# A quarter block of rows subtracted by GpSimd in four instructions of 128x512 instead of one of 128x2048

## The chip, the cores and the metric

The kernel runs on one core of one Trainium2 chip. A core has TensorE (PE in the profile, its weight loads PEld), VectorE (DVE), ScalarE (ACT), GpSimd (POOL) and SyncE (SP), which here only issues transfers. The metric is the time of one execution on the device in microseconds (us), lower is better. The profile shows one execution on the one core that is used.

## The reference, cut to what matters

```python
x = x + _L0_xattn_ref(_layernorm(x), ctx_4096)    # the stage that fills the time
x = x + _L0_attn_ref(_layernorm(x), Wq, bq, Wk, bk, Wv, bv)
x = x + _L0_ffn_ref(_layernorm(x), ...)

def _L0_xattn_ref(query, key):                    # query (1, 256, 2048), key (1, 25088, 2048)
    a = jnp.einsum('bqd,bkd->bqk', query, key)
    e = jax.nn.softmax(a, axis=-1)
    c = jnp.einsum('bqk,bkd->bqd', e, key)
```

All is float32. The cross-attention reads its 25088 context rows twice in effect: once as keys (with the feature axis on the partitions) and once as values (rows on the partitions).

## The kernel before

**Splitting.** Each float32 operand of TensorE is split in a high part (a cast to fp32r) and a low part (the operand minus its high part), and each product is three matmuls: high by high, low by high, high by low (lines L960 to L962).

**Blocks.** The context is walked in 49 blocks of 512 rows with a running softmax. A block has two uses, and each has its own tiles:

- *Scores.* The block comes as `quart` (two halves `h` of 4 transfers of 512 KB each). For each of 16 chunks of 128 features, DVE transposes to `tr` (L733), ACT casts to `ch_hi` (L517), DVE subtracts to `ch_lo` (L737), and PE does 6 matmuls (2 tiles of 128 queries, 3 products each). `tr`, `ch_hi` and `ch_lo` are rings of 4 slots; a slot of `ch_hi`/`ch_lo` is written again when PE has used it.
- *Weighted rows.* The same block comes again as `raw`, in 4 pieces of 512 features (1024 KB each) through 2 buffers. ACT casts piece `j` to `nat_hi` (L540), and GpSimd subtracts to `nat_lo` (L459, the changed line). PE multiplies the transposed probabilities with them in 8 steps of 12 matmuls; DVE adds each step's result to `acc` (L775). The 8 steps use 2 PSUM banks in turn, so the third step waits until DVE has added the first.

**Order.** The order is written by hand. PE does the weighted rows of a block in the middle of the next block's scores, after chunk 6. On ACT the four casts of pieces stand after chunk 10 (three of them) and after chunk 11 (the last). DVE runs 3 chunks ahead: between its subtractions it transposes, takes the maximum of the scores (L754, L757) as soon as it gets to it, and subtracts for the probabilities (L667); then it rescales (L765, L767) and adds (L775). `following` says which chunk is transposed behind which subtraction: chunk 8, the first of the second half of `quart`, behind the subtraction of chunk 6.

**Transfers.** All of them but one pair stand in one SP queue, in program order, and each waits at its head:

```python
for j in range(2):
    sp.wait_ge(nat_ready[j + 2], turn.times(1, 1))
    load_rows(j, rows_src(j))
if not turn.first and not turn.last:
    second_half()
```

`nat_ready[j]` is what GpSimd's subtraction of piece `j` increments. So the load of `raw` piece 1 of the next block (L318), and behind it in the queue the four loads of the second half of `quart` (L325), wait for GpSimd's subtraction of piece 3. The second half waits for the transpose of chunk 15 too.

**GpSimd's other work.** In the first 16 rounds of two blocks GpSimd also adds up `Wq` over groups of heads: one load and, after the second block's piece 3, three additions of 128x512 (L472, L473, L475) and a store. Every second block of the first 33 thus has these three behind its piece 3.

Of the kernel before, what the change touches and what calls it, by code (L numbers as in the profile page):

```python
# [5 lines left out]
F32 = mybir.dt.float32  # L6
U32 = mybir.dt.uint32
ALU = mybir.AluOpType
# [20 lines left out]
def perceiver_block(nc, x, ctx, wq, bq, wk, bk, wv, bv, w_base, b_base, w_gate, lora_a, lora_b, out):  # L29
# [21 lines left out]
    KT = KB // P  # L51
# [34 lines left out]
    with ExitStack() as stack:  # L86
        def sem(name):
            return stack.enter_context(nc.semaphore(name))
# [10 lines left out]
        def put(at, name, shape, dt=F32):  # L99
            return nc.alloc_sbuf_tensor_at(name, shape, dt, offset=at)  # L100
# [15 lines left out]
        raw = put(at_raw, "raw", [P, 2, KT, BANK])  # L116
        quart = put(at_quart, "quart", [P, 2, RG, HALF])
        nat_hi = put(at_hi, "nat_hi", [P, PIECES, KT, BANK], F32R)
        nat_lo = put(at_lo, "nat_lo", [P, PIECES, KT, BANK], F32R)
# [102 lines left out]
        nat_ready = [sem(f"nat_ready{j}") for j in range(PIECES)]  # L222
# [84 lines left out]
        def in_pairs(eng, work, start=0, end=PAIRS):  # L307
            with eng.Fori(start, end) as i:
                for step in range(2):
                    work(Turn(i, step))  # L310
# [129 lines left out]
        @block.gpsimd  # L440
        def _(pool):
            pool.memset(ident[:, :], 0.0).then_inc(consts_set, 1)
            pool.memset(ones[:, :], 1.0).then_inc(consts_set, 1)
            pool.iota(iota8[:, :], [[1, EXPERTS]], base=0, channel_multiplier=0,
                      allow_small_or_imprecise_dtypes=True).then_inc(consts_set, 1)

            for parity in range(2):
                pool.memset(neg_max[:, parity, :], -LOWEST).then_inc(max_ready, 1)
            pool.memset(denom[:, :], 0.0).then_inc(denom_ready, 1)
            pool.wait_ge(consts_set, 3)  # L450
            pool.affine_select(out=ident[:, :], in_=ident[:, :], compare_op=ALU.not_equal, fill=1.0,
                               base=0, pattern=[[-1, P]], channel_multiplier=1).then_inc(consts, 1)
            for t in range(TT):
                pool.memset(acc[:, t, :], 0.0).then_inc(acc_updated, 1)

            def lo_piece(j, ready):

                pool.wait_ge(nat_hi_ready, ready)
                pool.tensor_tensor(nat_lo[:, j], raw[:, j % 2], nat_hi[:, j].bitcast(F32), ALU.subtract).then_inc(nat_ready[j], 1)  # L459

            def split_block(turn):
                for j in range(PIECES):
                    lo_piece(j, turn.times(PIECES, j + 1))

            split_block(FIRST)
            with pool.Fori(0, DC) as i:
                pool.dma_start(wq_in[:], wq[bass.ds(i * P, P)].rearrange("p d h -> p (d h)")).then_inc(wq_loaded, 16)
                for step in range(2):
                    split_block(Turn(i, step))
                w4 = wq_in[:].rearrange("p (n j) -> p n j", j=REP)  # L470
                pool.wait_ge(wq_loaded, i * 16 + 16)
                pool.tensor_tensor(w4[:, :, 0], w4[:, :, 0], w4[:, :, 1], ALU.add).then_inc(wq_half, 1)  # L472
                pool.tensor_tensor(w4[:, :, 2], w4[:, :, 2], w4[:, :, 3], ALU.add).then_inc(wq_half, 1)  # L473
                pool.wait_ge(wq_half, i * 2 + 2)
                pool.tensor_tensor(wq_out[:], w4[:, :, 0], w4[:, :, 2], ALU.add).then_inc(wq_summed, 1)  # L475
                pool.wait_ge(wq_summed, i + 1)
                pool.dma_start(wq_dram[bass.ds(i * P, P)], wq_out[:]).then_inc(wq_stored, 16)
                pool.wait_ge(wq_stored, i * 16 + 16)
            in_pairs(pool, split_block, DC, PAIRS)
            for turn in REST:  # L480
                split_block(turn)
            for j in range(PIECES):
                lo_piece(j, NB * PIECES + j + 1)
            pool.wait_ge(wq_stored, 16 * DC)

            pool.wait_ge(qkv_done, 3 * TT)
            pool.memset(v_t[:, :, :, :], 0.0).then_inc(v_zeroed, 1)
            pool.wait_ge(v_zeroed, 1)
            for j in range(2):
                pool.memset(v_t[DH * j:DH * (j + 1), :, :, (KVH + 1) * j + KVH], 1.0).then_inc(v_zeroed, 1)  # L490
# [712 lines left out]
```

## Time and profile before

| what | value |
|---|---|
| device time, median of 3 runs | 2737.11 us (2726.85 to 2743.08) |
| span of the profiled execution | 2735.8 us |
| PE busy | 2517.3 us, 92% |
| DVE busy | 1834.0 us, 67% |
| ACT busy | 1120.2 us, 41% |
| POOL busy | 1018.9 us, 37% |
| chain that ended last | PE 67%, DVE 15%, issue 8%, ACT 5%, DMA 3% |
| `nat_lo` on POOL (L459) | 200 instructions, 921.7 us |

The profiled execution's own device time is not listed apart from the others; its span, 2735.8 us, lies inside the range of the three times. Matmul records overlap, so PE's 92% does not mean that it works at its peak.

### The profile page before, as it was taken

What the parts mean: (1) busy time and instruction counts of PE and PEld (TensorE: products, weight loads), DVE (VectorE), ACT (ScalarE), POOL (GpSimd) and SP (SyncE); (2) the same over time, 40 slices, a digit from 0 to 9 for tenths busy, and PEclk for the clock granted to TensorE, in tenths of its full rate; (3) what the DMA queues carried; (4) which work ended last, traced back from release to release, by engine and by line L of the source; (5) the groups of instructions that cost most, each with busy time, mean ns of one, the idle gap of its engine ahead of it and who ended that gap; (6) DMA issues with size and microseconds to landing.
All of it is one profiled execution on the core that took longest, in us unless ns stands there. A gap on an engine that the chain in (4) does not pass through costs nothing.

```text
span 2735.8 us, 34584 instructions
## 1 busy us (share of the span) xinstructions
PE 2517.3 (92%) x11342; PEld 2044.4 (75%) x11342; DVE 1834.0 (67%) x2668; ACT 1120.2 (41%) x1569; POOL 1018.9 (37%) x296
## 2 busy tenths in 40 slices
PE   5999999999999999999999999999999999996789
PEld 3777777777777777777777777777777777765677
DVE  7767667676766767676675766767576676572568
ACT  3444344443444444444444444444344444331423
POOL 3254443535435353443534444242433435220000
PEclk8999999999999999999999999999999999998579
DMA  9767778687776867767676866767677676658237
GB/s 218 191 179 188 183 196 193 170 202 189 185 178 197 193 177 195 186 180 188 188 198 174 203 172 177 176 169 182 171 180 172 179 174 169 174 138 120 39 67 149
DMA packets 377510, 476.08 MB, mean 174 GB/s; under 512 B 48707, under 2 KB 265795, under 8 KB 374853
## 3 DMA queue, kind: packets, MB, share of 16 engines
q1 hardware_dynamic: 373894, 454.68, 68.1%
q0 software_dynamic: 3584, 20.97, 2.3%
q8 instruction: 20, 0.33, 0.1%
q14 instruction: 12, 0.10, 0.0%
HBM read 467.74 MB, written 7.86 MB: 174 GB/s over the span
## 4 chain that ended last, share of the span: by engine, by line
PE 67%; DVE 15%; issue 8%; ACT 5%; DMA 3%; SPq 1%; POOL 0%; ACTq 0%; DVEq 0%
PE ps L960 22%; PE ps L962 21%; PE ps L961 21%; DVE ch_lo L737 10%; ACT ch_hi L517 2%; ACT nat_hi L540 2%; DVE blk_max L754 1%; DMA raw<-in_L_attn_Wv_dram 1%; DVE tr L733 1%; DMA raw<-in_ctx_dram 1%; PE ps L969 1%; DMA q_t<-qk_dram 1%; SPq L325 1%; PE ps L990 1%; PE ps L1135 1%
## 5 line engine op out<-in xcount | busy, mean ns | idle before, releaser
L459 POOL TENSOR_TENSOR nat_lo<-raw,nat_hi 128x2048 fp32r<-128x2048 f32 x200 | 921.7, 4609 | 1269.5 <-ACT nat_hi L540 1269.5
L737 DVE TENSOR_TENSOR ch_lo<-tr,ch_hi 128x512 fp32r<-128x512 f32 x848 | 782.0, 927 | 168.0 <-ACT ch_hi L517 165.6
L960 PE MATMUL ps<-ch_hi,xt_hi 128*128 128x512 f32 x1696 | 697.0, 411 | 136.8 <-DVE ch_lo L737 134.3
L517 ACT CAST ch_hi<-tr 128x512 fp32r<-128x512 f32 x848 | 516.2, 620 | 743.3 <-DVE tr L733 372.6
L775 DVE SCALAR_TENSOR_TENSOR acc<-acc,alpha,ps 128x512 f32<-128x512 f32 x392 | 292.6, 747 | 583.2 <-PE ps L962 583.0
L962 PE MATMUL ps<-ch_hi,xt_lo 128*128 128x512 f32 x1696 | 675.4, 398 | 0.0
L961 PE MATMUL ps<-ch_lo,xt_hi 128*128 128x512 f32 x1696 | 675.1, 398 | 0.0
L540 ACT CAST nat_hi<-raw 128x2048 fp32r<-128x2048 f32 x208 | 397.3, 1910 | 620.4 <-PE ps L962 353.1
L960 PE MATMUL ps<-nat_hi,pt_hi 128*128 128x512 f32 x1568 | 610.9, 390 | 1.4 <-DVE pt_lo L667 1.4
L962 PE MATMUL ps<-nat_hi,pt_lo 128*128 128x512 f32 x1568 | 610.6, 389 | 0.0
L961 PE MATMUL ps<-nat_lo,pt_hi 128*128 128x512 f32 x1568 | 610.5, 389 | 0.0
L733 DVE STREAM_TRANSPOSE tr<-quart 128x512 f32<-128x512 f32 x848 | 588.6, 699 | 3.2 <-DMA quart<-in_ctx_dram 1.8
L960 PEld LDWEIGHTS ps<-ch_hi,xt_hi 128*128 128x128 f32 x1696 | 327.7, 193 | 240.4 <-DVE ch_lo L737 171.7
L962 PEld LDWEIGHTS ps<-ch_hi,xt_lo 128*128 128x128 f32 x1696 | 326.5, 193 | 72.0
L961 PEld LDWEIGHTS ps<-ch_lo,xt_hi 128*128 128x128 f32 x1696 | 328.3, 194 | 64.4 <-issue 0.7
L960 PEld LDWEIGHTS ps<-nat_hi,pt_hi 128*128 128x128 f32 x1568 | 294.8, 188 | 62.8 <-DVE pt_lo L667 1.6
L961 PEld LDWEIGHTS ps<-nat_lo,pt_hi 128*128 128x128 f32 x1568 | 294.8, 188 | 61.2
L962 PEld LDWEIGHTS ps<-nat_hi,pt_lo 128*128 128x128 f32 x1568 | 294.7, 188 | 61.2
L546 ACT ACTIVATE probs<-ps,neg_max 128x512 f32<-128x512 f32 x98 | 67.5, 689 | 98.0 <-DVE neg_max L757 98.0
L754 DVE TENSOR_REDUCE blk_max<-ps 128x1 f32<-128x512 f32 x98 | 65.4, 667 | 4.5 <-PE ps L962 4.4
L667 DVE TENSOR_TENSOR pt_lo<-ps,pt_hi 128x512 fp32r<-128x512 f32 x98 | 66.9, 683 | 1.6 <-ACT pt_hi L501 1.6
L969 PE MATMUL ps<-ident,probs 128*128 128x128 f32 x392 | 59.4, 274 | 3.0 <-ACT probs L546 1.9
(125 smaller groups left out, 913.4 us busy)
## 6 DMA issues: line engine op xcount, KB each, us to landing
quart<-in_ctx_dram SPq DMA_DIRECT2D x392, 512.0 KB, 9.0
raw<-in_ctx_dram SPq DMA_DIRECT2D x196, 1024.0 KB, 5.1
wq_in<-in_L_attn_Wq_dram POOLq DMA_DIRECT2D x16, 1024.0 KB, 5.5
quart<-in_L_ffn_W_base_dram SPq DMA_DIRECT2D x32, 512.0 KB, 8.6
wq_dram<-wq_out POOLq DMA_DIRECT2D x16, 256.0 KB, 8.6
raw<-in_L_attn_Wk_dram SPq DMA_DIRECT2D x4, 1024.0 KB, 5.3
raw<-wq_dram SPq DMA_DIRECT2D x4, 1024.0 KB, 5.4
raw<-in_L_attn_Wv_dram SPq DMA_DIRECT2D x4, 1024.0 KB, 16.7
```

The source lines that it names most:

```text
L459: pool.tensor_tensor(nat_lo[:, j], raw[:, j % 2], nat_hi[:, j].bitcast(F32), ALU.subtract).then_inc(nat_ready[j], 1)
L517: act.copy(ch_hi[:, c % RING_CH, :], tr[:, c % RING_TR, :]).then_inc(chunk_hi, 1)
L540: act.copy(nat_hi[:, j], raw[:, j % 2]).then_inc(nat_hi_ready, 1)
L546: act.activation(probs[:, q, :], ps[:, SCORE_BANK + TT * new + q, :], ACT.Exp, bias=neg_max[:, new, q:q + 1], accum_out=row_sum[:, q:q + 1 ...
L733: dve.transpose(tr[:, c % RING_TR, :].rearrange("p (r i) -> p r i", i=SQ), src).then_inc(chunk_transposed, 1)
L737: dve.tensor_tensor(ch_lo[:, c % RING_CH, :], tr[:, c % RING_TR, :], ch_hi[:, c % RING_CH, :].bitcast(F32), ALU.subtract).then_inc(chunk_s ...
L754: dve.tensor_reduce(blk_max[:, q:q + 1], ps[:, SCORE_BANK + TT * new + q, :], AX.X, ALU.max, negate=True).then_inc(blkmax_ready, 1)
L775: dve.scalar_tensor_tensor(piece, piece, alpha[:, q:q + 1], ps[:, out_bank(v, turn.over), :], ALU.mult, ALU.add).then_inc(acc_updated, 1)
L960: pe.matmul(out_, a_hi, b_hi, start=start, stop=False)
L961: pe.matmul(out_, a_hi, b_lo, start=False, stop=False)
L962: return pe.matmul(out_, a_lo, b_hi, start=False, stop=stop)
L969: last = pe.transpose(ps[:, bank, a * P:(a + 1) * P], src, ident[:, :])
```

## The change

```diff
             def lo_piece(j, ready):
 
                 pool.wait_ge(nat_hi_ready, ready)
-                pool.tensor_tensor(nat_lo[:, j], raw[:, j % 2], nat_hi[:, j].bitcast(F32), ALU.subtract).then_inc(nat_ready[j], 1)
+                for t in range(KT):
+                    last = pool.tensor_tensor(nat_lo[:, j, t], raw[:, j % 2, t], nat_hi[:, j, t].bitcast(F32), ALU.subtract)
+                last.then_inc(nat_ready[j], 1)
```

`KT` is 4. The same elements are read and written, and one semaphore increment follows the last of the four, as it followed the one. All 200 subtractions of GpSimd become 800. Nothing else is changed; behind this place the line numbers of the changed kernel are higher by 2.

On GpSimd (POOL), before, the end of the round of two blocks that also has the additions for `Wq`, from the subtraction of the last `nat_lo` piece to the store of the sum:

```order
L459 TENSOR_TENSOR nat_lo<-raw,nat_hi 128x2048
L471 ISA
L472 TENSOR_TENSOR wq_in<-wq_in 128x512
L473 TENSOR_TENSOR wq_in<-wq_in 128x512
L474 ISA
L475 TENSOR_TENSOR wq_out<-wq_in 128x512
```

On GpSimd after the change, the same place:

```order
L460 TENSOR_TENSOR nat_lo<-raw,nat_hi 128x512 x4
L473 ISA
L474 TENSOR_TENSOR wq_in<-wq_in 128x512
L475 TENSOR_TENSOR wq_in<-wq_in 128x512
L476 ISA
L477 TENSOR_TENSOR wq_out<-wq_in 128x512
```

The piece is now a row of four instructions (x4) with nothing between them, of the same size as the additions that follow. Nothing moved past anything else, and the other engines' order is as before.

## Rows read from the trace of the kernel before

**Rows 1.** Page, costliest groups: count, then busy us and mean ns.

```profile
L459 POOL TENSOR_TENSOR nat_lo<-raw,nat_hi 128x2048 fp32r<-128x2048 f32 x200 | 921.7, 4609 | 1269.5 <-ACT nat_hi L540 1269.5
L737 DVE TENSOR_TENSOR ch_lo<-tr,ch_hi 128x512 fp32r<-128x512 f32 x848 | 782.0, 927 | 168.0 <-ACT ch_hi L517 165.6
```

**Rows 2.** Waits, 85 to 2298 us: total us, times, longest us.

```profile
PE ps L960 <- DVE ch_lo L737: 110.5, 56, 2.3
...
DVE tr L733 <- DMA quart<-in_ctx_dram: 1.8, 5, 0.6
```

**Rows 3.** Timeline of POOL, one block: start us, duration us.

```profile
572.54 4.61 POOL L459 TENSOR_TENSOR nat_lo<-raw,nat_hi 128x2048 fp32r<-128x2048 f32 x1 [10.31 <-ACT nat_hi L540]
...
590.78 4.57 POOL L459 TENSOR_TENSOR nat_lo<-raw,nat_hi 128x2048 fp32r<-128x2048 f32 x1 [1.72 <-ACT nat_hi L540]
```

**Rows 4.** Timeline of DVE, the same block.

```profile
591.26 4.65 DVE L737 TENSOR_TENSOR ch_lo<-tr,ch_hi 128x512 fp32r<-128x512 f32 x1 [1.01 <-ACT ch_hi L517]
595.83 0.70 DVE L733 STREAM_TRANSPOSE tr<-quart 128x512 f32<-128x512 f32 x1
596.46 0.64 DVE L737 TENSOR_TENSOR ch_lo<-tr,ch_hi 128x512 fp32r<-128x512 f32 x1
597.03 0.69 DVE L733 STREAM_TRANSPOSE tr<-quart 128x512 f32<-128x512 f32 x1
...
603.63 0.64 DVE L754 TENSOR_REDUCE blk_max<-ps 128x1 f32<-128x512 f32 x1
...
611.03 0.70 DVE L733 STREAM_TRANSPOSE tr<-quart 128x512 f32<-128x512 f32 x1
...
616.10 0.75 DVE L775 SCALAR_TENSOR_TENSOR acc<-acc,alpha,ps 128x512 f32<-128x512 f32 x1
```

**Rows 5.** Timeline of PE around the stop in that block.

```profile
593.24 0.39 PE L962 MATMUL ps<-ch_hi,xt_lo 128*128 128x512 f32 x1
595.96 0.50 PE L960 MATMUL ps<-ch_hi,xt_hi 128*128 128x512 f32 x1 [2.33 <-DVE ch_lo L737]
```

**Rows 6.** Timeline, POOL and DVE where the additions for `Wq` follow a piece.

```profile
1216.99 4.57 POOL L459 TENSOR_TENSOR nat_lo<-raw,nat_hi 128x2048 fp32r<-128x2048 f32 x1 [1.79 <-ACT nat_hi L540]
1217.46 4.64 DVE L737 TENSOR_TENSOR ch_lo<-tr,ch_hi 128x512 fp32r<-128x512 f32 x1 [1.02 <-ACT ch_hi L517]
1221.52 1.60 POOL L472 TENSOR_TENSOR wq_in<-wq_in 128x512 f32<-128x512 f32 x1
...
1222.66 0.98 DVE L737 TENSOR_TENSOR ch_lo<-tr,ch_hi 128x512 fp32r<-128x512 f32 x1
...
1223.04 1.60 POOL L473 TENSOR_TENSOR wq_in<-wq_in 128x512 f32<-128x512 f32 x1
...
1224.19 0.98 DVE L737 TENSOR_TENSOR ch_lo<-tr,ch_hi 128x512 fp32r<-128x512 f32 x1
1224.72 1.46 POOL L475 TENSOR_TENSOR wq_out<-wq_in 128x512 f32<-128x512 f32 x1
```

**Rows 7.** Windows: length, busy per engine, granted clock, DMA share, GB/s.

```profile
85.00:2298.00 2213.00, 2098.89 (x9206) 1705.94 (x9205) 1508.88 (x2210) 943.10 (x1310) 936.44 (x263) 0.99 0.73 183
568.33:615.81 47.48, 45.03 (x202) 36.77 (x201) 32.32 (x49) 19.87 (x28) 18.41 (x4) 1.00 0.77 188
615.81:664.30 48.49, 45.72 (x202) 36.47 (x201) 33.35 (x49) 21.17 (x29) 24.02 (x9) 1.00 0.71 190
```

**Rows 8.** Line L765 (first step of a block's rescaling), 85 to 2298 us.

```profile
L765 DVE TENSOR_TENSOR denom_s<-denom,alpha x47: 146/151/156, 85.1 to 2297.9; 128x2 f32<-128x2 f32 x47
```

**Rows 9.** Timeline of SP behind GpSimd's piece 3: raw, then quart.

```profile
595.38 0.37 SPq L318 DMA_DIRECT2D raw<-in_ctx_dram  x1
596.69 15.43 SPq L325 DMA_DIRECT2D quart<-in_ctx_dram  x8
```

**Rows 10.** Line L325, 596 to 599 us: its issues and landings.

```profile
L325 SPq DMA_DIRECT2D quart<-in_ctx_dram x4: 333/348/695, 596.7 to 598.3; - x4
...
DMA to landing us min/median/max: 7.3/10.1/12.6
```

**Rows 11.** Windows while these transfers move, and just after.

```profile
597.00:609.00 12.00, 11.88 (x57) 9.66 (x56) 11.01 (x21) 6.71 (x16) 0.00 (x0) 1.00 1.07 253
609.50:610.50 1.00, 1.00 (x6) 0.83 (x5) 1.00 (x3) 0.52 (x1) 0.00 (x0) 1.00 0.11 20
```

**Rows 12.** Timeline of PE: first matmul of the rows, and of their third step.

```profile
612.39 0.39 PE L960 MATMUL ps<-nat_hi,pt_hi 128*128 128x512 f32 x1
...
617.84 0.39 PE L960 MATMUL ps<-nat_hi,pt_hi 128*128 128x512 f32 x1
```

**Rows 13.** Line L325 in another block; its raw was issued at 1509.9.

```profile
L325 SPq DMA_DIRECT2D quart<-in_ctx_dram x4: 334/378/1196, 1511.2 to 1512.8; - x4
...
DMA to landing us min/median/max: 7.7/10.8/13.4
```

**Rows 14.** Waits in the first pass, 30 to 86 us.

```profile
PE ps L960 <- DVE ch_lo L737: 14.7, 4, 5.7
```

**Rows 15.** Timeline of DVE in the second layer norm.

```profile
2406.27 2.62 DVE L692 TENSOR_TENSOR ln_b<-var_eps,ln_a 128x1 f32<-128x1 f32 x1
2408.92 4.45 DVE L693 TENSOR_TENSOR ln_a<-ln_b,std 128x1 f32<-128x1 f32 x1
```

**Rows 16.** Waits, 2404 to 2416 us.

```profile
PE ps L969 <- DVE x_nat L702: 4.9, 1, 4.9
```

## The prediction

> **What bounds the kernel now.** I read the page's costliest groups first. They show GpSimd's 200 subtractions at 4609 ns and an oddity on DVE: the mean of `ch_lo` is 927 ns [rows 1], though most of these last 0.64 us [rows 4]. Then the waits of the steady part: PE stops 56 times for `ch_lo`, 110.5 us in all [rows 2]. The timelines of one block show why. Piece 3 of GpSimd runs from 590.78 to 595.35 [rows 3]. DVE's subtraction for chunk 12 starts at 591.26 and lasts 4.65 us [rows 4]: it ends 0.55 us after GpSimd's, which is about its own work. Meanwhile PE has used up what was ready: no matmul starts between 593.24 and 595.96, where 0.23 us is the usual step, so 2.5 us are lost [rows 5]. The other three pieces of a block (the first at 572.54) lie beside PE's weighted rows, when DVE only adds results from PSUM and transposes.
>
> The row on which all turns is that DVE's two-input subtraction does not run beside GpSimd's. The Trainium skill says the same (SBUF — State Buffer, SBUF: two separate sides): the loser waits for the winner's whole instruction.
>
> Is PE's stop all that sets a block's length? A block lasts 47.48 us, and one with the additions for `Wq` 48.49 [rows 7]. In the latter DVE's three next subtractions last 0.98 instead of 0.65 us [rows 6], 1.0 us together, just the difference. So behind the stop DVE's series of transposes and subtractions up to the maximum (603.63, [rows 4]) sets the pace.
>
> **What it removes.** The subtraction for chunk 12 then waits for one quarter, not for the piece. A quarter is 4.57/4 = 1.14 us [rows 3]. Does DVE get in between two quarters? The additions for `Wq` are such a row of 128x512: DVE's subtraction runs behind the piece, behind L472 and behind L473, though the next GpSimd instruction was already there [rows 6]. Each pair takes 1.53 us (DVE from 1222.66 to 1224.19). A lone pair of transpose and subtraction takes 1.20 us (595.83 to 597.03, [rows 4]). So DVE comes from the start of piece 3 to the maximum in 1.14+0.54, then 3 x 1.53, 3 x 1.20 and a transpose of 0.6: 10.5 us, where it was 603.63-590.78 = 12.85. That is 2.4 us less for each block, and PE's own gap is 2.5. If nothing else were late, 46 blocks would give 110 us.
>
> **What it adds.** Piece 3 gets longer, since DVE now runs between its quarters: 1.14+3 x 1.53 = 5.75 us instead of 4.57. From below it is 4.57 (nothing added), from above 4.57+3 x 0.55 = 6.2 (DVE's work in full). I take 5.75, measured on instructions of this size, though their inputs are strided.
>
> **What is late next.** Behind piece 3 SP issues `raw`, at 595.38, then the second half of `quart`, from 596.69 [rows 9]. The last of it is issued at 598.3 and lands 12.6 us later, at 610.9 [rows 10]. The transfers are not idle meanwhile: the share is 1.07 from 597 to 609 us, and 0.11 behind that [rows 11]. So an earlier issue of `quart` alone helps little; landing follows the issue of `raw` by 15.5 us. The transpose that needs it starts at 611.03, at once, and from there DVE goes without a pause to its first addition, which ends at 616.85 [rows 4]. PE needs that for its third step at 617.84 [rows 12]. So this second route has only 0.9 us of slack today. Its length after the change: piece 3 5.75, issue 0.03, landing 15.5, DVE 5.95, semaphore 0.05, and from the third step of the rows (617.84, which is 5.45 behind the first at 612.39, [rows 12]) to the next piece 3, one block of 47.48 behind 590.78 at 638.26: 20.4. Sum 47.7 us. With today's 4.57 it is 46.5, which with the slack of 0.9 is the 47.48 seen.
>
> Two things that the slack hid now count. Landing is later in some blocks: 1512.8+13.4-1509.9 = 16.3 us [rows 13]; I add 0.2, the mean of a spread of which I know only the ends. And TensorE's granted clock is 0.99 over the stage [rows 7], short drops to the lower of its two levels; 1% of the 20.4 us that are PE's is 0.2. So a block is 48.1 us. Today's mean is (2297.9-85.1)/46 = 48.1 [rows 8]. **In the steady part the change gives back all that it gains**: PE's stop moves from chunk 12 to the third step of the rows. Terms: +0 (46 blocks).
>
> **Outside the steady part.** In the first pass PE stops 4 times for `ch_lo`, 14.7 us [rows 14]; the quarters would cut some 10 of it, but loads of `raw` are behind there too; I take 5. The last block has no second half of `quart` to wait for: 2.5. In the second layer norm two tiny two-input operations last 2.62 and 4.45 us under GpSimd's pieces [rows 15] and PE waits 4.9 us for what follows [rows 16]; with quarters they are done 5 us sooner: 4.9. Sum 12.4.
>
> **Cost of the extra 600 instructions where DVE does not contend.** Pieces 0 to 2 may each become longer by three dispatches. The nearest row is L472, issued at 1221.52, before the piece ends, and done 1.02 us after DVE's subtraction ended: no visible start-up. Piece 1 has about 1 us of slack before its `raw` load matters, so I take 0.
>
> Span 2735.8-12.4 = 2723; the median of the runs is 1.3 higher than the span: **2724 us**.
>
> **The rivals.**
> *B, the full gain.* Landing would have to follow less than the whole delay: the engines' share is not flat at the transfer's begin, and `quart` is issued 0.9 us sooner relative to `raw`. If all of that came off and more, DVE's route would rule: 2735.8-110-12.4 = 2613. Against it stands the share of 1.07 [rows 11]. Half of it (0.9 us a block) gives 2682. Chance 0.15.
> *C, no change in what it does.* GpSimd keeps the port over all four quarters, DVE waits 4.6 us as today: 2737. L472 and L473 speak against it [rows 6]; but they have a semaphore update each, the quarters have none. The Trainium skill says (GPSIMD Engine Reference, Instruction dispatch) that a GpSimd core starts the next instruction when its own share is done, without waiting for the others; by that rule the quarters could leave DVE no gap, and the time would be that of C. In the trace DVE got in. Chance 0.13.
> *D, slower.* Each boundary costs more than 0.4 us: with 0.7 each, piece 3 is 6.7 us, each block 0.95 longer, 44 us in all: 2767. It decides from a piece of about 6.3 us, where (6.3-5.75) x 46 = 25 eats the 12.4 and 13 more. For it: the upper bound is 6.2 even without any start-up, and a later `quart` shares the engines with the next block's first half, whose four issues are the second half of the eight in [rows 9] and come 2.4 us sooner. Chance 0.2.
> *A*, the forecast, has 0.52; it spans 2690 (landing 0.7 sooner) to 2755 (piece of 6.2, landing 0.2 later).
>
> **Chances.** About 0.5% (13.7 us) is what a measurement of this kernel can tell from no change; its three runs spread by 0.6%. A is at this bound: of its 0.52, 0.25 lies below, 0.21 within, 0.06 above. B is faster (0.15), C the same (0.12 and 0.01 faster), D slower 0.17, same 0.03. Faster 0.41, same 0.36, slower 0.23. The range leaves out B's far end and the worst of D: 2680 to 2765.
>
> **What would show it.** The longest `ch_lo` falls from 4.65 to some 1.7 us and the group's mean to about 700 ns; PE's 56 waits for `ch_lo` are gone. Four subtractions of piece 3 take 5.75 us from first start to last end (4.6: rival C; over 6.3: D). DVE's transpose waits for `quart` in nearly every block, about 3.5 us each, where it was 1.8 us in all, and PE stops some 2.5 us before the third step of the rows for `acc` (neither: rival B). I am wrong in a term if landing behind the issue of `raw` is not 15.5 us, and in the route if PE stops elsewhere.

## The result and the profile after

The changed kernel takes 2768.34 us (median of 4 runs, 2761.83 to 2774.35), the kernel before on the same chip 2733.70 us (4 runs, 2726.85 to 2743.08). The ratio is 1.0117, with a 95% interval of 1.0088 to 1.0146, so it is **slower by 1.2%**, clear of the noise; the medians differ by 34.6 us. The forecast was 2724 us within 2680 to 2765, so the result lies 3 us above its range. The profiled execution has a span of 2767.5 us, 31.7 us above that of before.

The page of the changed kernel, its costliest groups (count, busy us, mean ns, then idle time ahead and what ended it). Line numbers are higher by 2 than in [rows 1]:

```profile
L460 POOL TENSOR_TENSOR nat_lo<-raw,nat_hi 128x512 fp32r<-128x512 f32 x800 | 1080.6, 1381 | 1141.5 <-ACT nat_hi L542 1141.5
L739 DVE TENSOR_TENSOR ch_lo<-tr,ch_hi 128x512 fp32r<-128x512 f32 x848 | 687.2, 815 | 168.9 <-ACT ch_hi L519 167.0
```

DVE's `ch_lo` got cheaper by 95 us and GpSimd's `nat_lo` dearer by 159 us. Neither engine is the bound, so neither number is the answer. The waits of the steady part are (us in all, times, longest), against [rows 2]:

```profile
DVE tr L735 <- DMA quart<-in_ctx_dram: 138.3, 46, 4.3
...
PE ps L962 <- DVE acc L777: 89.0, 45, 3.3
...
PE ps L962 <- DVE ch_lo L739: 13.9, 46, 0.3
```

PE's stops for `ch_lo` shrank from 110.5 to 13.9 us, and 45 new ones for `acc`, 89.0 us, took their place. DVE waits 138.3 us for `quart`, where it waited 1.8. The timelines of one block show the route of the new wait. GpSimd, piece 3 (the view joins the four instructions in one row), against [rows 3]:

```profile
592.27 6.40 POOL L460 TENSOR_TENSOR nat_lo<-raw,nat_hi 128x512 fp32r<-128x512 f32 x4 [2.34 <-ACT nat_hi L542]
```

SP behind it, against [rows 9]:

```profile
598.69 0.37 SPq L318 DMA_DIRECT2D raw<-in_ctx_dram  x1
599.31 12.64 SPq L325 DMA_DIRECT2D quart<-in_ctx_dram  x8
```

DVE, first beside piece 3, then where it needs the second half of `quart`, against [rows 4]:

```profile
592.74 1.37 DVE L739 TENSOR_TENSOR ch_lo<-tr,ch_hi 128x512 fp32r<-128x512 f32 x1 [1.01 <-ACT ch_hi L519]
594.03 0.70 DVE L735 STREAM_TRANSPOSE tr<-quart 128x512 f32<-128x512 f32 x1
594.66 1.15 DVE L739 TENSOR_TENSOR ch_lo<-tr,ch_hi 128x512 fp32r<-128x512 f32 x1
...
614.25 0.71 DVE L735 STREAM_TRANSPOSE tr<-quart 128x512 f32<-128x512 f32 x1 [3.40 <-DMA quart<-in_ctx_dram]
...
619.32 1.40 DVE L777 SCALAR_TENSOR_TENSOR acc<-acc,alpha,ps 128x512 f32<-128x512 f32 x2
```

PE at the third step of the rows, against [rows 12]:

```profile
617.34 0.39 PE L964 MATMUL ps<-nat_hi,pt_lo 128*128 128x512 f32 x1
620.12 0.50 PE L962 MATMUL ps<-nat_hi,pt_hi 128*128 128x512 f32 x1 [2.40 <-DVE acc L777]
...
621.08 0.63 PE L962 MATMUL ps<-nat_hi,pt_hi 128*128 128x512 f32 x1
621.50 0.63 PE L963 MATMUL ps<-nat_lo,pt_hi 128*128 128x512 f32 x1
```

The `ch_lo` beside piece 3 lasts 1.37 us instead of 4.65. Piece 3 lasts 6.40 us instead of 4.57, `raw` is issued 0.02 us behind it, the last transfer of `quart` lands 15.46 us behind that, DVE starts at once and PE at 620.12. From 621.08 on the matmuls follow each other by 0.42 us instead of 0.23. The windows (length, busy us of PE, PEld, DVE, ACT, POOL, granted clock, DMA share, GB/s) of the steady part, of two neighbouring blocks and of the stretch behind PE's stop, against [rows 7]:

```profile
85.00:2330.00 2245.00, 2125.99 (x9181) 1691.37 (x9179) 1419.73 (x2200) 938.50 (x1309) 1075.84 (x814) 0.99 0.72 180
570.65:619.04 48.39, 45.57 (x200) 36.54 (x200) 30.54 (x49) 20.45 (x29) 21.50 (x16) 1.00 0.76 194
619.04:669.28 50.24, 47.74 (x200) 37.48 (x200) 31.62 (x49) 20.42 (x30) 27.08 (x21) 0.97 0.70 173
620.20:623.40 3.20, 3.20 (x9) 2.55 (x10) 0.53 (x1) 0.00 (x0) 3.20 (x3) 0.59 0.97 174
```

The last row has a granted clock of 0.59, mostly the lower of TensorE's two levels (1.2 instead of 2.4 GHz), right behind the stop. The first step of each block's rescaling, against [rows 8], gives the mean of 46 blocks as (2331.3-78.3)/46 = 48.98 us, where it was 48.1:

```profile
L767 DVE TENSOR_TENSOR denom_s<-denom,alpha x47: 146/149/154, 78.3 to 2331.3; 128x2 f32<-128x2 f32 x47
```

### The profile page after: what moved, and what is told of

Same layout as the page of the kernel before. It is cut to its first block, busy times and chain, and to the rows that moved or that the text cites. A ratio compares the mean times of both kernels' runs of the same rounds, so it can differ in the third digit from the quotient of the medians.

```text
span 2767.5 us, 35184 instructions
## 1 busy us (share of the span) xinstructions
PE 2542.2 (92%) x11342; PEld 2027.8 (73%) x11342; DVE 1730.4 (63%) x2668; ACT 1117.2 (40%) x1569; POOL 1177.5 (43%) x896
## 4 chain that ended last, share of the span: by engine, by line
POOL 39%; issue 39%; DMA 9%; PE 8%; DVE 2%; SPq 2%; ACT 1%; POOLq 0%; DVEq 0%; ACTq 0%
POOL nat_lo L460 36%; DMA wq_dram<-wq_out 5%; PE ps L962 2%; PE ps L964 2%; PE ps L963 2%; DMA raw<-in_L_attn_Wv_dram 1%; DMA raw<-in_ctx_dram 1%; DMA q_t<-qk_dram 1%; POOL wq_in L474 1%; POOL wq_in L475 1%; POOL wq_out L477 1%; SPq L386 1%; SPq L325 1%; PE ps L992 1%; PE ps L1137 1%
## 5 line engine op out<-in xcount | busy, mean ns | idle before, releaser
L460 POOL TENSOR_TENSOR nat_lo<-raw,nat_hi 128x512 fp32r<-128x512 f32 x800 | 1080.6, 1381 | 1141.5 <-ACT nat_hi L542 1141.5
L739 DVE TENSOR_TENSOR ch_lo<-tr,ch_hi 128x512 fp32r<-128x512 f32 x848 | 687.2, 815 | 168.9 <-ACT ch_hi L519 167.0
L962 PE MATMUL ps<-ch_hi,xt_hi 128*128 128x512 f32 x1696 | 688.2, 406 | 29.1 <-DVE ch_lo L739 26.5
L962 PE MATMUL ps<-nat_hi,pt_hi 128*128 128x512 f32 x1568 | 626.3, 399 | 93.0 <-DVE acc L777 91.6
L963 PE MATMUL ps<-ch_lo,xt_hi 128*128 128x512 f32 x1696 | 665.0, 392 | 0.0
L964 PE MATMUL ps<-ch_hi,xt_lo 128*128 128x512 f32 x1696 | 664.6, 392 | 0.0
L964 PE MATMUL ps<-nat_hi,pt_lo 128*128 128x512 f32 x1568 | 620.6, 396 | 0.0
L963 PE MATMUL ps<-nat_lo,pt_hi 128*128 128x512 f32 x1568 | 620.3, 396 | 0.0
L962 PEld LDWEIGHTS ps<-ch_hi,xt_hi 128*128 128x128 f32 x1696 | 320.1, 189 | 145.3 <-DVE ch_lo L739 81.2
L971 PEld LDWEIGHTS ps<-ident,probs 128*128 128x128 f32 x392 | 45.1, 141 | 45.9 <-issue 34.3
```

Of the source, the lines that this page charges most:

```text
L460: last = pool.tensor_tensor(nat_lo[:, j, t], raw[:, j % 2, t], nat_hi[:, j, t].bitcast(F32), ALU.subtract)
L739: dve.tensor_tensor(ch_lo[:, c % RING_CH, :], tr[:, c % RING_TR, :], ch_hi[:, c % RING_CH, :].bitcast(F32), ALU.subtract).then_inc(chunk_s ...
L962: pe.matmul(out_, a_hi, b_hi, start=start, stop=False)
L963: pe.matmul(out_, a_hi, b_lo, start=False, stop=False)
L964: return pe.matmul(out_, a_lo, b_hi, start=False, stop=stop)
L971: last = pe.transpose(ps[:, bank, a * P:(a + 1) * P], src, ident[:, :])
```

## Where the 31.7 us are

The spans differ by four stretches, cut at the first steps of the rescaling. The first comes 6.8 us sooner (78.3 for 85.1). The 47 intervals behind it are longer by 39.0 us. The last block is shorter by 4.0 us. What follows is longer by 3.5 us. That last one is not the change's for sure: `e4_before_quart_ahead` (below), which leaves GpSimd's code as it was, is longer by 3.4 us there too.

For the 47 intervals I summed the prediction's own route, averaged over the 47 blocks from the records of the instructions that begin and end each leg.

| leg of the route, us | predicted | measured, mean | difference |
|---|---|---|---|
| piece 3 of GpSimd | 5.75 | 6.41 | +0.66 |
| its end to DVE's transpose (issue and landing) | 15.73 | 15.53 | -0.20 |
| DVE to the end of its first addition, and semaphore | 6.00 | 5.88 | -0.12 |
| PE's third step of the rows to the next piece 3 | 20.60 | 21.15 | +0.55 |
| one block | 48.08 | 48.97 | +0.89 |

The last leg has two values: 20.6 us in 30 blocks and 22.2 us in 16 (one at the end has 21.3). The 16 are those in which the clock fell behind PE's stop at the third step.

## The experiments

The first theory (Theory 1 in the expectations) is this table: a block is as long as the route from piece 3 over `raw`, `quart`, DVE and the third step. Against it stood that the 600 additional instructions cost time wherever they are (Theory 2; the chain on the page of the changed kernel puts 36% of the span on this line), that the place of the load does not matter, and that the quarters' own form makes them long.

### Piece 3 alone, and all but piece 3

`e1_only_piece3` splits only piece 3, `e2_all_but_piece3` the other three (with `n = KT if j == 3 else 1`):

```diff
-for t in range(KT):
-    last = pool.tensor_tensor(nat_lo[:, j, t], raw[:, j % 2, t], ...)
+n = 1 if j == 3 else KT
+for t in range(0, KT, n):
+    last = pool.tensor_tensor(nat_lo[:, j, t:t + n], raw[:, j % 2, t:t + n], ...)
```

> Only piece 3 is issued in quarters, pieces 0 to 2 whole. Theory 1 (route: GpSimd's piece 3, raw load, second half of quart, DVE's transposes, third step of the rows): piece 3 is all that counts, so the time is that of the changed kernel, 2768 us, within 8. Theory 2 (600 more instructions cost time wherever they stand, as the chain of the changed kernel's page has it, which puts 36% on this line): only a quarter of the extra is left, about 2743 us.

> Pieces 0 to 2 in quarters, piece 3 whole. Theory 1: as before the change, 2734 us within 8, with the stop of 2.5 us at chunk 12 in every block and no wait of DVE's transpose for quart. Theory 2: three quarters of the extra, about 2760 us.

Piece 3 alone gives 2778.25 us, a ratio of 1.0159 (1.0117 to 1.0202), 2 us beyond what was expected, though its interval overlaps that of the whole change; the other three give 2728.17 us, 0.9973 (0.9952 to 0.9993), within it. The waits of piece 3 alone are those of the whole change:

```profile
DVE tr L736 <- DMA quart<-in_ctx_dram: 137.2, 45, 3.8
...
PE ps L963 <- DVE acc L778: 91.5, 45, 2.8
```

Without it they are those of before:

```profile
PE ps L963 <- DVE ch_lo L740: 112.6, 56, 2.3
DVE tr L736 <- DMA quart<-in_ctx_dram: 3.4, 10, 0.7
```

So 150 of the 200 pieces are not to blame: the loss sits in the 50 pieces 3, and the 450 extra instructions of the others cost nothing (0.3% faster, and in the steady part of the profiled executions the same, 48.16 us a block against 48.14).

### The transfer's place in the queue

If the route decides, it can be cut at SP: `quart`'s second half needs nothing of piece 3, it only stands behind `raw` in the queue. `e3_quart_ahead` exchanges them in the changed kernel, `e4_before_quart_ahead` in the kernel before.

```diff
 for j in range(2):
+    if j == 1 and not turn.first and not turn.last:
+        second_half()
     sp.wait_ge(nat_ready[j + 2], turn.times(1, 1))
     load_rows(j, rows_src(j))
-if not turn.first and not turn.last:
-    second_half()
```

> The changed kernel with one exchange in SP's queue: the four loads of the second half of quart stand ahead of the load that waits for GpSimd's piece 3. Theory 1: the landing no longer hangs on piece 3, PE's stop at the third step of the rows goes, and DVE's own series rules: from piece 3 to the maximum 11.2 us instead of 12.85, so 45.9 us for a block and 46.9 for one with the additions, 46 x (48.1-46.2) = 87 us less than before the change, some 2640 us. Theory 2: still 2768.

> The kernel before, with the same exchange in SP's queue. Theory 1: the landing is hidden there but for a few late blocks, so 2734 us, at most 10 less. A rival, that the order of the loads alone is worth something (the transfers run better in this order): as large a gain as in the changed kernel, 90 to 130 us.

With the quarters it takes 2637.65 us, 0.9637 (0.9599 to 0.9676); without them 2737.83 us, 1.0007 (0.9989 to 1.0024). DVE's wait for `quart` and PE's for `acc` are gone from the list of waits. PE is left with small ones, for `ch_lo` and 12.3 us in all for the probabilities:

```profile
PE ps L962 <- DVE ch_lo L739: 14.2, 47, 0.3
```

The clock is 1.00 over the stage up to 2100 us:

```profile
85.00:2100.00 2015.00, 1986.51 (x8738) 1595.34 (x8736) 1386.86 (x2093) 896.94 (x1247) 1034.76 (x782) 1.00 0.76 192
```

Piece 3 still lasts 6.41 us, the mean block 46.15. This is what the change is worth when the transfer is not behind it: 100 us against the exchange alone. The exchange alone is worth nothing, because before the change PE's stop at chunk 12 and DVE's series behind it set the pace. Each half of the pair is useless or harmful, both together gain 3.6%.

### Why a quarter lasts longer than a fourth of a piece

`e5_add` changes the operation of the quarters to an addition; it leaves out the low part, since `nat_lo` then holds another value. `e9_loose_forms` adds 20 instructions of 128x512 in an idle stretch of GpSimd near the end, in five forms: with the output and inputs of the quarters, with a float32 output, with both inputs in one tile, with inputs at a stride of four elements, and in place. (Two fills stand ahead of them and one later load waits for them; only their durations are read.)

```diff
-last = pool.tensor_tensor(..., ALU.subtract)
+last = pool.tensor_tensor(..., ALU.add)
```

```diff
+for _ in range(4):
+    for dst, one, two, op in ((m_r[:, :], m_a[:, 0], m_b[:, :], ALU.subtract),
+                              (m_f, m_a[:, 0], m_b[:, :], ALU.subtract),
+                              (m_f, m_a[:, 0], m_a[:, 1], ALU.subtract),
+                              (m_f, w[:, :, 0], w[:, :, 1], ALU.subtract),
+                              (m_a[:, 0], m_a[:, 0], m_a[:, 1], ALU.subtract)):
+        pool.wait_ge(m_step, steps)
+        pool.tensor_tensor(dst, one, two, op).then_inc(m_step, 1)
+        steps += 1
```

> The changed kernel with an addition in place of the subtraction in all 800 quarters (nat_lo then holds another value; nothing else is left out). The prediction took 1.53 us for a quarter with DVE's subtraction from the additions for Wq; the subtractions of the changed kernel take 1.71. If the operation makes the difference, the piece 3 of this kernel lasts 1.1+3x1.53 = 5.7 us instead of 6.4 and the time is some 30 us less than 2768. If the operands do (fp32r output, strides, in place), it stays at 6.4 and 2768.

> The changed kernel, with 20 further subtractions of 128x512 on GpSimd in its idle time near 2440 us, each behind the one before, four of each of five forms: (1) two tiles in, fp32r out; (2) two tiles in, float32 out; (3) two slots of one tile in, float32 out; (4) the same with a stride of four elements, as in the additions for Wq; (5) like 3 but written over its input. In the runs so far a lone quarter lasts 1.28 us, a lone addition for Wq 1.12. If the output type makes the difference, form 1 lasts 1.28 and the others 1.12; if the two tiles do, forms 1 and 2 last 1.28; if the stride does, form 4 alone 1.12. Their durations are read, not the time.

One execution each: 2771.93 us and 2764.76 us (kernel before: 2740.08 and 2740.93). In the first, the quarters last as long as subtractions do (ns, minimum, median, maximum):

```profile
L460 POOL TENSOR_TENSOR nat_lo<-raw,nat_hi x800: 1256/1291/2266, 34.0 to 2459.2; 128x512 fp32r<-128x512 f32 x160
```

Piece 3 lasts 6.41 us here too, so the operation makes no difference. In the second, the line that issues the added instructions:

```profile
L506 POOL TENSOR_TENSOR m_r<-m_a,m_b x8: 1269/2242/3231, 2464.1 to 2491.3; 128x512 fp32r<-128x512 f32 x4, 128x512 f32<-128x512 f32 x4
L506 POOL TENSOR_TENSOR m_r<-m_a x8: 1133/1272/1470, 2466.8 to 2496.0; 128x512 f32<-128x512 f32 x8
L506 POOL TENSOR_TENSOR m_a<-m_a x4: 1269/1281/1620, 2469.4 to 2497.5; 128x512 f32<-128x512 f32 x4
```

The first two rows mix two forms each. The strided ones (half of the second row) last 1.13 to 1.18 us in three of their four uses. All others last 1.27 to 1.29 us where DVE does not interfere, whatever the output type and whether the inputs are in one tile or two; the longest of the first row, 3.2 us, stand beside subtractions of 128x2048 by DVE. So contiguous 128x512 takes 1.28 us and four make 5.0 us, not 4.6 (the whole piece 0 of a block: 4.61 us). My price of the first quarter was a fourth of the piece, 1.14 us, and that of the others came from the additions for `Wq`, whose inputs have that stride and which last 1.11 us where DVE leaves them alone (`e8_eighths3_quart_ahead`): wrong neighbours by 0.14 and 0.17 us.

### Halves

`e6_halves` issues every piece as two of 128x1024, `e7_halves_quart_ahead` does the same with SP's exchange.

```diff
-for t in range(KT):
-    last = pool.tensor_tensor(nat_lo[:, j, t], raw[:, j % 2, t], ...)
+n = 2
+for t in range(0, KT, n):
+    last = pool.tensor_tensor(nat_lo[:, j, t:t + n], raw[:, j % 2, t:t + n], ...)
```

> Two instructions of 128x1024 for each piece. Theory 1 (a block is the longer of two routes): piece 3 is 4.57+0.61 = 5.2 us, since each boundary added 0.61 in the changed kernel; the transfer route is then 41.8+5.2 = 47.0 us, DVE's series to the maximum 12.3 us instead of 12.85, which gives 46.9. So 1.1 us less for a block than before, 2734-50-10 = 2675 us within 12. Theory 2 (every further instruction costs): between 2734 and 2768.

> Halves, and the loads of quart ahead of the load behind piece 3. Theory 1: only DVE's series is left, 46.9 us a block, so hardly better than halves alone, 2670 us within 12, and worse than quarters with the same exchange (2638).

They take 2697.52 us, 0.9856 (0.9829 to 0.9882), and 2684.81 us, 0.9819 (0.9787 to 0.9850). Both are above what was expected, by 10 and 3 us beyond its edge. The last half of piece 2, undisturbed, and piece 3, which has one boundary:

```profile
622.25 2.41 POOL L461 TENSOR_TENSOR nat_lo<-raw,nat_hi 128x1024 fp32r<-128x1024 f32 x1
626.20 5.20 POOL L461 TENSOR_TENSOR nat_lo<-raw,nat_hi 128x1024 fp32r<-128x1024 f32 x2 [1.54 <-ACT nat_hi L543]
```

That is 1.2 us less than with quarters, and the mean block is 47.39 us. This is enough to leave the route no more than short waits (DVE waits for `quart` 21.5 us in all up to 2100 us), but DVE's subtractions beside the two halves last 2.48 and 2.25 us and PE stops for them, 1.15 us at the longest and some 1.6 us a block in all, so the transfer's place matters little (47.32 us). Between halves and quarters neither is better in itself: with the old queue halves win, with the new one quarters do.

### Eighths of piece 3

An eighth of 128x256 lasts about as long as DVE's transpose (0.70 us from the first eighth's start to the next one's, and 0.70), so DVE's subtraction need not wait for it. `e10_eighths3` splits only piece 3, in eight, `e8_eighths3_quart_ahead` adds the exchange.

```diff
+if j == 3:
+    for t in range(2 * KT):
+        part = slice(t % 2 * BANK // 2, (t % 2 + 1) * BANK // 2)
+        last = pool.tensor_tensor(nat_lo[:, j, t // 2, part], raw[:, j % 2, t // 2, part],
+                                  nat_hi[:, j, t // 2, part].bitcast(F32), ALU.subtract)
+else:
+    last = pool.tensor_tensor(nat_lo[:, j], raw[:, j % 2], nat_hi[:, j].bitcast(F32), ALU.subtract)
```

> Piece 3 in eighths as in the fastest kernel so far, but with SP's loads in their old order. Theory 1: piece 3 lasts 9.1 us and the loads of quart wait for it: 41.8+9.1 = 50.9 us a block, 46 x 2.8 = 129 us more than before, less 12 outside, and TensorE's clock falls behind the long stop in a third of the blocks or more, 26 to 75 us: 2860 to 2925 us. A rival, that finer parts help in either order since DVE never waits: under 2734.

> Pieces 0 to 2 whole, piece 3 in eight instructions of 128x256, loads of quart ahead. Theory 1: piece 3 gets longer, some 9 to 10 us, but nothing waits for it; DVE waits at most 0.6 us at each subtraction and mostly less, its series is 9.5 to 10.5 us instead of 11.2, and a block nears PE's own 45.0 to 45.5 us: 2600 to 2625 us. Rival (DVE loses more to eight boundaries than it gains): over 2645.

The same GpSimd code gives 2974.45 us, 1.0862 (1.0842 to 1.0883), behind the old queue, and 2566.44 us, 0.9374 (0.9349 to 0.9399), behind the new one. GpSimd and DVE in the fast one:

```profile
504.26 9.07 POOL L462 TENSOR_TENSOR nat_lo<-raw,nat_hi 128x256 fp32r<-128x256 f32 x8 [1.90 <-ACT nat_hi L547]
```

```profile
504.73 0.82 DVE L744 TENSOR_TENSOR ch_lo<-tr,ch_hi 128x512 fp32r<-128x512 f32 x1 [1.02 <-ACT ch_hi L524]
505.47 0.70 DVE L740 STREAM_TRANSPOSE tr<-quart 128x512 f32<-128x512 f32 x1
506.10 0.65 DVE L744 TENSOR_TENSOR ch_lo<-tr,ch_hi 128x512 fp32r<-128x512 f32 x1
```

Piece 3 takes twice as long as whole, its eighths following each other by 1.20 us, which is DVE's own step of a transpose and a subtraction; yet DVE's second subtraction has its undisturbed 0.65 us. PE is busy in the whole of the stretch, at full clock:

```profile
85.00:2100.00 2015.00, 2015.00 (x9064) 1669.05 (x9063) 1297.30 (x2167) 930.72 (x1285) 1119.20 (x577) 1.00 0.78 198
```

A mean block is 44.5 us. That is better than expected by 34 us: I had not counted on PE without any stop. In the slow one the 9 us lie in the route. Its waits:

```profile
DVE tr L740 <- DMA quart<-in_ctx_dram: 354.2, 45, 8.3
...
PE ps L967 <- DVE acc L782: 280.3, 45, 6.7
```

Its windows of the stage and of a stretch behind one stop:

```profile
85.00:2480.00 2395.00, 2114.75 (x9044) 1728.62 (x9043) 1294.12 (x2166) 924.54 (x1284) 1112.43 (x576) 0.93 0.66 167
614.20:617.70 3.50, 3.50 (x10) 2.76 (x9) 0.00 (x0) 0.00 (x0) 3.50 (x1) 0.50 1.06 277
```

I had expected 2860 to 2925, so it is 50 us beyond. The mean block is 53.0 us. A block of the quarters without a drop, 48.4, and the longer piece, 9.07-6.41, make 51.1; the clock falls at all 46 stops, which are 5.8 to 7.7 us long, and the other 2 us are put down to it: the leg from PE's third step to the next piece 3 is 22.6 us on average, where it is 20.6 in the blocks of the quarters without a drop. Two results 408 us apart from one and the same GpSimd code are the strongest test of the theory: what the length of piece 3 costs is decided by the load behind it.

## Why the prediction was wrong

**What bounds the kernel now**, right. The stop at chunk 12 was the one that set the pace, DVE's blocked subtraction was its cause: with the transfer out of the way, removing it gives 100 us (`e3_quart_ahead` against `e4_before_quart_ahead`), where the text had 110. So does the series of DVE behind it: there a block with the additions for `Wq` is still 0.9 us longer than one without (46.75 and 45.84 us).

**What it removes**, right in kind, and rival C is out; in size DVE comes from the start of piece 3 to the maximum in 11.1 us where the text had 10.5, for the reason told in the next paragraph. DVE gets in at each boundary, 0.55 us of its own work behind the quarter's end. The Trainium skill (SBUF — State Buffer, SBUF: two separate sides) calls the shared port pair an exclusive lock, held for the whole instruction; the trace agrees, since cutting the instruction cut DVE's time from 4.65 to 1.37 us. Rival C was a handover from quarter to quarter that leaves DVE no gap. The prediction named beside it what the Trainium skill (GPSIMD Engine Reference, Instruction dispatch) says, that a GpSimd core starts the next instruction when its own share is done. No piece 3 of the trace shows DVE shut out: between its quarters the starts lie 1.70 us apart, where they lie 1.25 apart without DVE.

**What it adds**, the step that failed. It had 1.14+3 x 1.53 = 5.75 us and an upper bound of 6.2; measured are 6.41. Of the 0.66 us, 0.45 is four lone quarters at 1.25 (from start to start) instead of 1.14, since a fourth of a piece is not the price of an instruction of a fourth. The rest is contention, 0.45 us a boundary (1.70 less 1.25) where I had 0.39 (1.53 less 1.14), and rounding. The upper bound was wrong for the same reason: it added DVE's work to 4.57, where four lone quarters, 5.0, would have given 6.65. Over 46 blocks the 0.66 us are 30 us.

**What is late next**, right in the route, and in that the wait moves to `quart` and `acc`, stop for stop: DVE's 46 waits for `quart` are 3.0 us each (3.5 forecast), PE's 45 for `acc` 2.0 us (2.5 forecast). Landing plus issue was 15.53 instead of 15.73 us (a gain of 9 us in all), DVE's leg 0.12 shorter (6 us). **The clock term was too small**: I had 20.4 us of PE at a mean clock, 0.2 us. The mean clock of the stage is the same as before, 0.99, but the drop has moved. Before, it came at the stop at chunk 12, in 16 blocks too, where DVE's series hides a part of it; two such stretches, windows of the kernel before:

```profile
356.20:358.20 2.00, 2.00 (x6) 1.51 (x6) 2.00 (x4) 0.50 (x2) 1.92 (x2) 0.50 0.92 332
308.50:310.50 2.00, 2.00 (x6) 1.52 (x6) 2.00 (x4) 0.59 (x1) 0.00 (x0) 0.50 1.03 384
```

There a block with a drop is 1.15 us longer than one without (48.65 against 47.50 us from piece 3 to piece 3), and with the additions for `Wq` only 0.16 (48.64 against 48.48). Now it comes within the rows, where nothing but PE sets the pace, and 16 x 1.6 = 26 us count in full. This leg is 0.55 us longer than I had it: 0.56 from the drops, and 0.2 for blocks without one (20.6 against 20.4; PE's first matmuls behind a stop follow each other more slowly, 620.12, 620.47, 620.71), less the 0.2 that I had allowed. That is another 25 us. The four differences, 0.89 us, make 42 us over 47 intervals; less the 3 by which the forecast's 48.08 lay below the 48.14 of before, that is the 39 seen.

**Outside the steady part**, half right: the first pass gave 6.8 us (5 forecast), the last block 4.0 (2.5). The layer norm did what was forecast, against [rows 15]:

```profile
2433.04 0.52 DVE L694 TENSOR_TENSOR ln_b<-var_eps,ln_a 128x1 f32<-128x1 f32 x1
2433.59 1.22 DVE L695 TENSOR_TENSOR ln_a<-ln_b,std 128x1 f32<-128x1 f32 x1
```

But the 4.9 us did not arrive: behind the matmuls that follow, PE is 0.65 us ahead of before, counted from the rescaling of the last block. PE stops elsewhere instead:

```profile
2453.18 0.50 PE L962 MATMUL ps<-nat_hi,xt_hi 128*128 128x512 f32 x1 [3.61 <-POOL nat_lo L460]
...
2459.10 0.50 PE L962 MATMUL ps<-nat_hi,xt_hi 128*128 128x512 f32 x1 [1.31 <-POOL nat_lo L460]
```

Here GpSimd's own pieces are what PE waits for. It comes to them sooner, and they have grown: the last four pieces take 21.9 us together where they took 19.4. This is the same mistake once more: the cost of the quarters was set to nothing where I looked only at DVE's gain. It is read from the traces, and no run was made for it; the two that split only some of the pieces fit it. With piece 3 alone the stop of 4.9 us stays and one for `nat_lo` of 1.9 us is new; with the other three the 4.9 us are gone and two for `nat_lo`, of 1.4 and 2.3 us, take their place. In all this part was 3.5 us longer where the forecast had 4.9 less, but as said above it differs by as much between kernels that are alike there.

**Cost of the extra instructions**, right in the steady part for pieces 0 to 2 (`e2_all_but_piece3`), though each of them got longer, 5.03 instead of 4.61 us; wrong at the end as just told.

**The rivals.** D held the case, with 2767 us and the point of decision at a piece of about 6.3 us. It was given 0.2, because I took the bound of 6.2 for firm. Its mechanism (each boundary over 0.4 us) is right in direction: 6.41-4.57 = 1.84 us over three boundaries is 0.6 each; its other argument, that a later `quart` shares the engines with the next block's loads, was not seen, since landing was shorter. That D's time was hit to about 1 us is partly luck: it came from a piece of 6.7 us, and with the 6.41 measured the same sum gives some 2754; the clock's term, which D did not have, and the part behind the last block made up for the rest.

## What to carry to other kernels

Price the split of an instruction with a lone instruction of the new size and of the same access pattern, not with a fraction of the long one, and make the upper bound from that. When a split lets a waiting engine in, the split instruction ends later, so look at who waits for its end: here a transfer in program order that needed nothing of it, and exchanging two queue entries turned a loss of 1.2% into a gain of 3.6%. A stop of PE has two prices, its own length and the clock behind it, and the second was smaller here where the work behind the stop waits for somebody anyway.

## What the runs showed of the hardware

- GpSimd's two-input subtraction of contiguous float32: 128x2048 4.61 us, 128x1024 2.41, 128x512 1.28 (1.25 from start to start). With inputs at a stride of four elements 128x512 took 1.11 to 1.18 us, less than contiguous ones. Why is open.
- With DVE's two-input subtraction waiting at each boundary, quarters follow each other by 1.70 us, and eighths take 9.07 us for eight. DVE got in even when GpSimd's next instruction was already there, with a semaphore update on the one before (the additions for `Wq`) or without one (the quarters). A boundary thus costs 0.45 us over the lone spacing, with halves too (5.20 us against 4.75); how that comes out of DVE's own 0.55 us of work was not separated.
- The clock fell to its lower level at stops of PE: in the kernel before at 16 of 47 stops, all of 2.3 us (idle time); in the changed kernel at 16 of the 46 at the third step, which were 1.8 to 3.3 us long, while the other 30 were 1.3 to 2.6 us long; in `e10_eighths3` at all 46, of 5.8 to 7.7 us, and there it began while PE still stood; up to 2100 us at none in the runs `e3_quart_ahead`, `e6_halves`, `e7_halves_quart_ahead` and `e8_eighths3_quart_ahead`, where no stop in this stretch is over 1.2 us. Which of the stops of about 2 us bring it, the records do not tell.
